# Window attention and a routed expert layer on one core: early gate steps redistributed, the second band's affine sooner, tokens written into the experts' bank by ScalarE

## The reference

```python
x = x + conv_ref(ln_c(x))      # instance norm, qkv, 8x8 windows, 4 heads, softmax, projection
t = to_tokens(x)               # (8, 4096, 32)
t = t + ffn_ref(ln_t(t))       # router softmax over 8 experts, the best 2, weights renormalised
x = from_tokens(t)
```

## Time and profile before

| | |
|---|---|
| time, median of 3 runs | 382.94 us (381.27 to 383.5) |
| time of the profiled execution | 381.23 us |
| its span, first to last instruction | 379.3 us |
| TensorE busy (matmul) | 333.4 us, 88% |
| VectorE busy | 327.5 us, 86% |
| ScalarE busy | 274.8 us, 72% |
| GpSimd busy | 163.6 us, 43% |
| mean granted clock of TensorE | 0.976 |

### The profile page before, as it was taken

The page is one execution under the profiler, slowest core; times in us unless marked ns, Lnnn a source line. Parts: engine busy times, 40 slices in busy tenths (PEclk is TensorE's granted clock), DMA queues, the critical chain, the costliest instruction groups (busy, mean ns, idle before and its releaser), DMA issues.

```text
span 379.3 us, 12902 instructions
## 1 busy us (share of the span) xinstructions
PE 333.4 (88%) x5494; PEld 176.7 (47%) x5494; DVE 327.5 (86%) x422; ACT 274.8 (72%) x477; POOL 163.6 (43%) x191
## 2 busy tenths in 40 slices
PE   7999889999999868989989998989988878858895
PEld 2556556666656534655655654546542212111221
DVE  2599988998998975999998896899898999999884
ACT  3668768779878865787877987876765785566763
POOL 8610000221222120378545212068759448957653
PEclk9999999999999996999999999999999998898999
DMA  7700011011010000101101101075222653773482
GB/s 297 334 3 3 3 31 29 3 31 29 3 32 29 4 14 17 29 2 31 29 3 30 32 2 29 21 174 118 49 65 62 162 129 78 166 182 83 118 210 94
DMA packets 13385, 26.19 MB, mean 69 GB/s; under 512 B 1680, under 2 KB 3856, under 8 KB 12944
## 3 DMA queue, kind: packets, MB, share of 16 engines
q1 hardware_dynamic: 12752, 23.60, 23.7%
q10 hardware_dynamic: 576, 1.77, 1.2%
HBM read 5.96 MB, written 4.19 MB: 27 GB/s over the span
## 4 chain that ended last, share of the span: by engine, by line
PE 50%; DVE 22%; ACT 8%; issue 7%; POOL 6%; DMA 5%; SPq 0%; POOLq 0%; DVEq 0%; ACTq 0%
PE psum L689 13%; PE psum L708 7%; PE psum L674 6%; DVE neg_max L1309 4%; PE psum L716 4%; PE psum L658 3%; PE psum L592 3%; PE psum L869 3%; DVE window_work L1312 3%; PE psum L487 2%; DMA stage<-in_x 2%; PE psum L640 2%; DVE window_work L1466 2%; DVE o_tok L1320 2%; PE psum L859 1%
## 5 line engine op out<-in xcount | busy, mean ns | idle before, releaser
L369 POOL TENSOR_TENSOR o_norm<-o_tok,o_rden 128x128 f32<-128x128 f32 x64 | 25.4, 419 | 169.2 <-DVE o_rden L1322 169.2
L1013 ACT ACTIVATE probs<-psum 128x512 f32<-128x512 f32 x128 | 74.7, 596 | 23.8 <-PE psum L689 23.1
L689 PE MATMUL psum<-weights_sb,window_work 128*128 128x128 f32 x512 | 81.2, 286 | 9.4 <-ACT k_sb L989 5.5
L1309 DVE TENSOR_REDUCE neg_max<-psum 128x16 f32<-128x1024 f32 x64 | 76.8, 1199 | 9.1 <-PE psum L674 9.1
L1312 DVE TENSOR_TENSOR window_work<-psum,neg_max 128x1024 f32<-128x1024 f32 x64 | 78.4, 1225 | 2.2
L689 PEld LDWEIGHTS psum<-weights_sb,window_work 128*128 128x128 f32 x512 | 55.4, 142 | 40.1 <-issue 16.0
L708 PE MATMUL psum<-probs,v_cols 128*32 128x64 f32 x2048 | 52.4, 226 | 0.4 <-DVE o_tok L1320 0.2
L708 PEld LDWEIGHTS psum<-probs,v_cols 128*32 128x32 f32 x2048 | 34.1, 110 | 30.2 <-issue 15.6
L996 ACT ACTIVATE stage<-k_sb,weights_sb 128x512 f32<-128x512 f32 x64 | 44.2, 723 | 0.0
L674 PE MATMUL psum<-stage 32*64 32x256 f32 x1024 | 35.9, 386 | 7.0 <-DVE window_work L1312 4.3
L1320 DVE STREAM_TRANSPOSE o_tok<-psum 128x512 f32<-128x512 f32 x32 | 22.8, 712 | 14.5 <-PE psum L708 14.5
(11 more groups left out here) (143 smaller groups left out, 618.4 us busy)
## 6 DMA issues: line engine op xcount, KB each, us to landing
stage<-act_all SPq DMA_DIRECT2D x36, 256.0 KB, 4.4
out<-v_cols SPq DMA_DIRECT2D x16, 256.0 KB, 2.1
stage<-in_x SPq DMA_DIRECT2D x3, 1024.0 KB, 13.3
x_moved<-x_cur SPq DMA_DIRECT2D x14, 192.0 KB, 2.4
gate_rows<-gate_parts SPq DMA_DIRECT2D x16, 128.0 KB, 2.9
x_moved<-x_cur SPq DMA_DIRECT2D x14, 64.0 KB, 2.2
weights_sb<-weights ACTq DMA_DIRECT2D x1, 811.5 KB, 13.9
stage<-in_x SPq DMA_DIRECT2D x1, 768.0 KB, 6.0
```

Of the source, the lines that this page charges most:

```text
L369: last = pool.tensor_tensor(o_norm[:, hf, :, p * 16:p * 16 + 16].rearrange("p g (b d) -> p g b d", b=2), t[:, p * 8:p * 8 + 8, :].rearrang ...
L689: last = nc.tensor.transpose(bank[TURN_BANKS[v % 2]][:, b * P:b * P + P], heads.rearrange("p h k -> p (h k)"), const["c_ident"][:, :])
L1013: nc.scalar.activation(probs[:, w % 4, :], bank[TURN_BANKS[w % 2]][:, :], ACT.Exp).then_inc(exp_done, 1)
L1309: nc.vector.tensor_reduce(m_t, t, AX.X, ALU.max, negate=True).then_inc(max_done, 1)
```

## The change

Five things are changed.

- Quads 0 and 1 get their own order of gate steps: 17, 18, 19, 20 stand ahead of 16. Steps 2, 19 and 20 go from VectorE to GpSimd. Step 2 is done by GpSimd in chunk 7 (and 13), behind `divide(m - 1, 1)`. VectorE's steps 17 and 18 move from the end of chunk 9 (15) to the place of step 15, between the halves of that chunk; step 24 moves from chunk 10 (and the experts' stage) to the end of chunk 9 (15). GpSimd does 19, 20, 16, 21, 22, 23 in one go in chunk 9 (15), and the copies 25 and 28 and steps 26, 27 and 29 each come half a chunk or a chunk sooner. `gate_exps` stays.
- VectorE's `instance_affine(1)` moves from the end of chunk 6 to behind the first shift of its half 1, and ScalarE's `x_cur` of chunk 8 from the start of chunk 7 to the end of chunk 6.
- TensorE's `queries_keys(m + 1)` moves ahead of one `weigh` (window 5 of chunk m - 1).
- `combine` goes. In all chunks ScalarE writes the tokens into the bank ahead of the experts and copies the result out behind them. `open_bank`, two small matmuls ahead of the last `weigh`, opens bank 6 for that.
- `bias` no longer starts a bank, and waits for the tokens in all chunks.

```diff
GATE_OPS = 30
+        EARLY_ORDER = (*range(16), 17, 18, 19, 20, 16, *range(21, GATE_OPS))
...
-        PRESET_FIRST = 2
...
+        def past(quad, n):
+
+            return (EARLY_ORDER.index(n) if quad < EARLY and n < GATE_OPS else n) + ONE
...
@@ GpSimd @@
             def gates(quad, n):
 
-                pool.wait_ge(gate_step[quad], n + ONE)
+                pool.wait_ge(gate_step[quad], past(quad, n))
                 w = spaces[quad]
-                if n == 5:
+                if n == 2:
+                    pool.wait_ge(raw_done, quad + 1)
+                    follow(pool.tensor_scalar(w.logit, std_two[:, quad % 2, :], const["c_rb"][:, 0:1], None, ALU.mult))
+                    one = pool.tensor_tensor(w.logit, w.logit, raw_logits[:, :], ALU.add)
+                elif n == 5:
...
+                elif n == 19:
+                    one = pool.tensor_tensor(small[:, p_best, :], small[:, near, :], small[:, rden, :], ALU.mult)
+                elif n == 20:
+                    one = pool.tensor_tensor(small[:, p_second, :], small[:, e_gap, :], small[:, p_best, :], ALU.mult)
...
-            EARLY_STEPS = (((5, 6), (8, 9)), ((11, 12, 13, 14), (16,)), ((21, 22, 23), (26, 27)), ((29,), ()))
+            EARLY_STEPS = (((), (2,)), ((5, 6), (8, 9)), ((11, 12, 13, 14), (19, 20, 16, 21, 22, 23)), ((26, 27), (29,)))
...
-                    k = m - (6 * quad + 8)
+                    k = m - (6 * quad + 7)
...
-                    if h == 3:
-                        early(CHUNKS + 1, 0)
...
@@ TensorE, chunk @@
                         turn(m - 1, NW - 1)
+                        queries_keys(m + 1)
                         weigh(*before, NW - 3)
-                        queries_keys(m + 1)
                         weigh(*before, NW - 2)
...
             def bias(c):
 
-                if c < PRESET_FIRST:
-                    wait_past(pe, summed, c - 1)
-                else:
-                    pe.wait_ge(preset, c + 1 - PRESET_FIRST)
-                if c == 1:
-                    pe.wait_ge(x2_done, CHUNKS + X2)
+                pe.wait_ge(preset, c + 1)
...
-                                 start=(c < PRESET_FIRST), stop=False, skip_group_check=True)
+                                 start=False, stop=False, skip_group_check=True)
...
+            def open_bank():
+
+                pe.wait_ge(exp_done, (CHUNKS * NW - 1) + EXP)
+                for half in range(2):
+                    last = nc.tensor.matmul(bank[6][:, half * 2 * P:half * 2 * P + 2 * P], gate_sel[0:32, 0:P],
+                                            gate_sel[0:32, 0:2 * P], start=(half == 0), stop=(half == 1),
+                                            skip_group_check=True)
+                last.then_inc(bank_opened, 1)
+
...
             weigh(CHUNKS - 1, 1, NW - 2)
+            open_bank()
             weigh(CHUNKS - 1, 1, NW - 1)
...
@@ ScalarE @@
                     if (k, hf) == (1, 1):
                         gate_exps(quad)
+                    if (k, hf) == (2, 0):
+                        gate_copies(quad, 25)
                     if (k, hf) == (2, 1):
-                        gate_copies(quad, 25)
-                    if (k, hf) == (3, 0):
                         gate_copies(quad, 28)
...
-                    if hf == 0 and m + 1 == BANDS:
-                        current(m + 1)
...
                         keep_projection(m - 1)
+                    if hf == 1 and m + 2 == BANDS:
+                        current(m + 2)
...
             def preset_bank(c):
 
-                act.wait_ge(summed, c + 1 - PRESET_FIRST)
-                act.wait_ge(x2_done, c + 1 + X2)
+                if c >= 2:
+                    act.wait_ge(summed, c - 1)
+                act.wait_ge(x2_done, (CHUNKS if c == 1 else c + 1) + X2)
...
             exps(CHUNKS - 1, NW - 1)
+            act.wait_ge(bank_opened, 1)
+            preset_bank(0)
             for c in range(CHUNKS):
                 for eh in range(2):
                     copy_gates(c, eh)
+                    if (c, eh) == (0, 0):
+                        early_gates(CHUNKS, 0)
+                    if (c, eh) == (1, 0):
+                        preset_bank(1)
                     if eh == 1 and c >= 1:
-                        if c - 1 >= PRESET_FIRST:
-                            write_out(c - 1)
+                        write_out(c - 1)
...
@@ VectorE @@
-                dve.wait_ge(gate_step[quad], n + ONE)
+                dve.wait_ge(gate_step[quad], past(quad, n))
...
-            EARLY_STEPS = {(6, 8): (0, 1), (7, 8): (2, 3, 4), (8, 1): (7,), (8, 8): (10,), (9, 1): (15,),
-                           (9, 8): (17, 18, 19, 20), (10, 1): (24,)}
+            EARLY_STEPS = {(6, 8): (0, 1), (7, 8): (3, 4), (8, 1): (7,), (8, 8): (10,), (9, 1): (15, 17, 18), (9, 8): (24,)}
...
                     shift(m, hf, 0)
+                    if hf == 1 and m == BANDS - 2:
+                        instance_affine(1)
                     if not first:
                         turn_back(m - 1, hf)
...
-                        elif m == BANDS - 2:
-                            instance_affine(1)
                         early(m, 8)
...
-                    if eh == 0 and 1 <= c <= PRESET_FIRST:
-                        combine(c - 1)
-                    if (c, eh) == (0, 1):
-                        early(CHUNKS, 1)
                     steps(c, eh)
```

More of the change, by code:

```diff
@@ L199, in metaformer_block @@
         preset = sem("preset")
+        bank_opened = sem("bank_opened")
         summed = sem("summed")
@@ L1149, in write_out @@
                 act.wait_ge(y_step, c * 2 + 2)
-                if c == PRESET_FIRST:
-                    act.wait_ge(summed, PRESET_FIRST)
                 wait_past(act, stored[c % OUTS], c // OUTS * 16)
@@ L1181, in _ @@
                         early_gates(CHUNKS, 1)
-                    if (c, eh) == (1, 1):
-                        early_gates(CHUNKS + 1, 0)
                     if eh == 0 and c + REP_FIRST < CHUNKS:
@@ L1438, in _ @@
                 chunk(m)
-            def combine(c):
-                dve.wait_ge(y_step, c * 2 + 2)
-                nc.vector.tensor_tensor(
-                    out_sb[:, c, :].rearrange("p (y win x) -> p win y x", win=NW, y=WS),
-                    bank[6 + c % 2][:, :].rearrange("p (win y x) -> p win y x", win=NW, y=WS),
-                    act_all[:, c * CHUNK:c * CHUNK + CHUNK].rearrange("p (win y x) -> p win y x", win=NW, y=WS),
-                    ALU.add).then_inc(summed, 1)
             divide(CHUNKS - 1, 1)
```

## The result

The changed kernel takes 389.49 us (median of 4 runs, 386.06 to 391.75), the kernel before 382.11 us beside it (4 runs, 381.14 to 383.5): a ratio of 1.0192 with a 95% interval of [1.0144, 1.0241], 7.4 us slower. The forecast was 386.9 us in a range of 381.5 to 391.5. The profiled execution of the changed kernel is the longest of its four, 391.75 us; the profiled one of before took 381.23 us. So the two traces differ by 10.5 us, 3.1 us more than the medians do.

What follows compares the result with a forecast made beforehand. TensorE (88% busy) and VectorE (86%) were taken to bound it by their order of work, VectorE in the experts' stage. Terms -1.0 - 4.3 - 1.3 + 4.0 + 5.1 + 1.3 + 1.8 - 1.65 = +3.95 on 382.94: 386.9 us, range 381.5 to 391.5.

Steps and rivals of the forecast that it cites:

- Part 1: Attention chunks 5, 6, 11 and 12: earlier queries_keys lets a weigh cover the 0.25 us key-copy wait, -1.0 us.
- Part 2: Crossing into the second image group: queries_keys waits 1.9 us in place of 4.0, scores sooner, -4.3 us (-5.0 to -2.1).
- Part 3: Chunks 7 and 13: gate step 2 on idle GpSimd frees 0.65 us of VectorE each time, -1.3 us.
- Parts 4 and 5: Chunks 9 and 15: VectorE's step 17 waits for ScalarE's exp of the gap, holding shift and turn, +4.0 and +5.1 us.
- Part 6: Behind the waits in chunks 9 and 15: TensorE's clock falls to half rate, +1.3 and +1.8 us.
- Part 7: Experts' stage: VectorE loses two combines and step 24, -1.65 us (bounds -2.5 and -0.5).
- (A): Rival: as forecast but the clock falls nowhere, crossing -5.0, sum +0.15, 383.1 us; chance 0.2.
- (B): Rival: experts' stage leaves its low-clock stretches once VectorE is relieved, up to 4.5 us, 378.6 us; chance 0.15.
- (C): Rival: all goes to the worse end, crossing -2.1 and clock behind the waits +5.5, 391.5 us; chance 0.1.

Runs made afterwards that it cites:

- all gate steps as before: Changed kernel with the gate steps back in the places of the kernel before; band, order and bank stay as changed: 374.58 us, 0.9799.
- band and order alone: Kernel before with only the second band sooner and queries_keys one weigh earlier: 376.72 us, 0.9855.
- step 2 alone: Changed kernel with gate steps put back except step 2, which stays on GpSimd; band, order and bank as changed: 373.86 us, 0.9792.
- the kernel with the filler: Changed kernel with four extra fp32 matmuls on TensorE in its waits ahead of turn(9, 4) and turn(15, 4): 384.40 us, 1.0069.
- step 2 alone, again: Second measurement of the changed kernel with gate steps put back except step 2 on GpSimd: 374.15 us, 0.9782.
- step 2, filler, again: Second measurement of the step-2-alone kernel with two extra fp32 matmuls ahead of gate_pair(9, 0, 0): 374.4 us, 0.9785.
- step 2, filler: Step-2-alone kernel with two extra fp32 matmuls ahead of gate_pair(9, 0, 0) in the experts' stage: 372.6 us, 0.9773.
- exp sooner, bank undone: Changed kernel with ScalarE's exp of the gap half a chunk sooner, and bank, bias and combine as before: 376.25 us, 0.9831.
- step 2, bank undone: Step-2-alone kernel with the tokens of chunks 0 and 1 added by VectorE as in the kernel before: 376.15 us, 0.9832.
- gates alone: Kernel before with the redrawn gate steps and nothing else: 393.17 us, 1.0285.
- exp sooner: Changed kernel with ScalarE's exp of the gap half a chunk sooner, in half 0 of chunk 9 (15): 376.82 us, 0.9852.

## Why the prediction came out as it did

The sign and the range were right, and so was the mechanism that it called decisive. The sum came 2.6 us short (386.9 against 389.49). By the differences it is 3.4 us short, +3.95 foreseen and +7.4 measured: the forecast started from 382.94, and the kernel before measured 382.11 with its fourth run. One term is behind it, that of the experts' stage, which had the wrong sign. The others add up to +5.6 as foreseen and to about +5.8 by the traces (-1.0, -5.1, -1.5, +4.4, +5.4 and +3.6), with no error above 0.8 us in one of them.

**Part 1, queries and keys (-1.0).** Right. The waits for k_sb fall from 5.5 us in 13 to 0.9 us in 3, but most of them were no loss. From the first reduce of chunk 0 to that of chunk 6 it is 82.03 us against 82.34, 0.3 us less, and chunks 10 to 14 take 73.31 us with all gate steps as before, against 74.04, 0.7 us less: 1.0 us in all, as foreseen, and far from the 3.5 of the upper bound.

**Part 2, second band (-4.3).** The mechanism is right, with the wait at 2.09 us where 1.9 was worked out and scores at 144.00 where 144.8 was. The size depends on the execution. From chunk 6 to chunk 8 band and order alone gain 5.4 us (32.47 against 37.85), with the clock up, against the -5.0 of one end. In the changed kernel it is 37.85 - 31.99 = 5.9 us, of which about 0.75 us are step 2's. But the clock does not always stay up. The very same kernel, step 2 alone, was profiled twice; the first window is the first profile's, the second that of the other one:

```profile
140.00:143.40 3.40, 3.39 (x80) 1.73 (x64) 3.34 (x5) 2.30 (x4) 0.00 (x0) 1.00 0.00 0
```
```profile
140.40:143.80 3.40, 3.39 (x69) 2.39 (x70) 3.36 (x5) 1.26 (x2) 0.00 (x0) 0.68 0.00 0
```

From chunk 6 to chunk 8 these took 31.71 and 33.41 us, so the half rate costs 1.7 us. It was there in 4 of the 11 profiled executions with the new band, and the length of the wait ahead of queries_keys does not tell them apart (1.79, 1.81, 1.83 and 2.04 us with it, 1.75 to 2.26 us without). The chip may: all three executions on one chip had it, one of the three on a second, none of the four on a third, nor the changed kernel, whose chip is not on record (the two profiles of step 2 alone are from different chips). That was not tested. The value between the two ends is thus no execution in between, but stands for two kinds of them; that it fits the median is luck.

**Part 3, step 2 (-1.3).** By the traces about 0.75 us each time, so 1.5 us where it stands. By the medians 0.7 us, or less in the second measurement (374.58 against 373.86 and 374.15). The cause is right; how much reaches the end, the medians can't tell.

**Parts 4 and 5, the waits (+4.0 and +5.1).** Right, and this is where the forecast was made. Step 17 waits 4.34 us (about 4.0 foreseen) and 4.71 us (4.4), the turns 5.19 (4.9) and 5.80 (5.6). Without the clock, by the kernel with the filler, chunk 9 costs 20.01 - 15.62 = 4.4 us and chunk 15 21.98 - 16.61 = 5.4 us. The turn in chunk 9 was foreseen at 187.9 and came at 181.68 because chunk 9 started 6.5 us sooner; the forecast had kept the times of before and priced the gain apart, which adds up as long as no wait sits against a fixed time. The next reduce started 188.48 - 167.15 = 21.33 us behind the first one. Of the 4.4 us against 4.0, 0.3 us are in the exp of the gap: step 17 was foreseen 11.02 us behind the chunk's first reduce (184.7 - 173.68) and came at 11.35, so the 0.25 us of part 1 did not reach ScalarE here. Step 24 was priced with a wait of 0.5 us for GpSimd. Without the half rate it waits 0.79 us; in the changed kernel, at 187.90, it doesn't wait, only because the half rate had held divide back.

**Part 6, the clock (+1.3 and +1.8).** The half rate came with both waits, and began 1.7 to 1.8 us before their ends. It cost 1.3 us in chunk 9 and 2.3 us in chunk 15, where 1.8 was taken. The range for both together ran from 0 to 5.5, and 3.6 us were measured. The 1.3 was half of a bound and a little more, not a working, and the 1.3 measured are 2.2 us of delay less 0.9 us that came back behind it, most of it at step 24: that they agree is luck. The rule of the Trainium skill (TensorE: Matmul & The Clock Gate, Part 1), that idle time brings the half rate back, held for these two waits, in both kernels that have them without a filler. The price that was put beside it, all matmuls behind the wait at half rate, did not: the clock was back to 0.76 on average in 185.0 to 188.4.

**Part 7, experts' stage (-1.65).** This is the step that failed. In the profiled executions the stage takes 104.7 us against 99.4, +5.3. Since the profiled one is the longest run of its four, the medians give a better estimate, if the time ahead of the gate_pair is the same in all executions: less the 1.8 us outside the span and the time of the gate_pair, 382.11 - 1.8 - 279.95 = 100.4 us before and 389.49 - 1.8 - 285.26 = 102.4 us after, +2.0. Against the forecast that is a miss of 3.65 us. The relief itself is not what failed: the new bank, with the two combines, brings 2.0 and 2.1 us in two comparisons of three. Step 24's share, 0.65 us, was not measured alone. What the sum lacked is that something is lost there at the same time, and it is no part of the new bank: band and order alone, whose experts' stage has the same code as before, lengthens it as well, from 100.4 to 376.72 - 1.8 - 273.15 = 101.8 us by the same estimate.

Two things go with it. One is the clock. The windows from 60 to 70 us behind the first gate_pair, in the kernel before, in band and order alone, and in the changed kernel:

```profile
339.95:349.95 10.00, 8.20 (x46) 1.82 (x46) 9.27 (x14) 6.89 (x12) 8.61 (x7) 0.83 0.40 88
```
```profile
333.15:343.15 10.00, 8.70 (x37) 2.18 (x40) 8.57 (x14) 5.15 (x9) 8.38 (x7) 0.51 0.37 81
```
```profile
345.26:355.26 10.00, 9.20 (x38) 2.04 (x38) 8.57 (x14) 5.84 (x10) 7.88 (x7) 0.50 0.38 85
```

All three lie in the same work, and VectorE, which sets the pace there, does 8.57 us of it in place of 9.27 when the clock is at 0.50. Over the whole stage, us at half rate (within the span) and length of the stage, one profiled execution each:

```
before                      11.4    99.4
step 2 alone                15.1   101.2
step 2 alone, again         17.1   101.8
step 2, filler, again       20.5   101.8
changed, filler in waits    20.5   101.7
band and order              22.0   102.6
step 2, filler              22.2   101.1
exp sooner, bank undone     23.9   104.7
all gate steps as before    23.9   103.1
step 2, bank undone         25.4   104.6
gates alone                 27.3   104.9
exp sooner                  29.2   102.9
changed                     32.7   104.7
```

A microsecond at half rate goes with about 0.25 us more (5.3 us for 21.3), with a scatter of up to 1.7 us either way. The four runs of the changed kernel say the same for one kernel: mean clocks of 0.941, 0.945, 0.956 and 0.964 with 391.75, 390.11, 388.86 and 386.06 us, in order. In the 25 executions of the kernel before that were measured beside the experiments (mean clocks of 0.962 to 0.986, 379.94 to 383.74 us) a straight line through them gives about 0.15 us. But the clock does not account for all of it. At the same mean clock, 0.964, the changed kernel's shortest run takes 386.06 us and the kernel before 381.69 to 382.95. And two runs of band and order alone, at 0.986, have about 10.5 us at half rate in their whole span, while their stage comes to 100.4 and 101.0 us by the estimate above, against 99.4 in the kernel before with 11.4 us. The other thing is one wait, VectorE for the tokens of a late chunk. In the kernel before and in band and order alone:

```profile
DVE window_work L1463 <- DMA stage<-act_all: 1.2, 2, 0.9
```
```profile
DVE window_work L1477 <- DMA stage<-act_all: 2.6, 1, 2.6
```

In the changed kernel it is 0.6 us, so it can't be the cause there. In the other versions it is 1.8 to 3.4 us, and the 3.4 are in the gates alone, whose attention stage is the longest of all, as well as in the changed kernel with the filler: it does not go with the length of the attention stage. Why there is more half rate behind some versions stays open. Two half-rate stretches lie at like places in all thirteen traces, somewhere between 31 and 45 and between 56 and 72 us behind the first gate_pair, a third between 85 and 97 in nine of them, and they vary in length between executions of the same kernel; one attempt to take one away changed the time by nothing that can be seen. What lengthens the stage is thus not found: that the clock is a cause and not only a companion is argued, not shown.

**The rivals.** (A), the clock falls nowhere, is excluded for the two new waits by the windows, and holds for the crossing in 7 of 11 profiles. (B) hung on the experts' stage leaving its low stretches once VectorE is relieved: the opposite came, 32.7 us in place of 11.4. (C) named the worse ends of parts 2 and 6; 2.6 of the 4.6 us that separate it from the forecast came, but by way of part 7, whose upper bound of -0.5 was too low. That the measured time still lies within the range is luck: the room at its upper end was there for parts 2 and 6, and part 7 used it. A bound from the work removed does not bound a stage in which other things can change with it. The bounds were not added up whole either: the low end takes part 1 at -1.0, although its own bound was -3.5, and leaves out the 0.5 us less of part 4.

## What to carry to other kernels

When a step is drawn forward on one engine, look up when each of its inputs is produced on the others, and move the producer too: here the exp of the gap came half a chunk too late, and that one line decides between 389.5 and 376.8 us. Price what is queued behind the waiting step rather than the step, and add a term for the clock where TensorE will wait as long as it did here (5.19 and 5.80 us). And price each part alone: of the four, the redrawn gate steps never paid as a whole, while step 2 alone with the new band, order and bank gives 374 us, 0.978 of the kernel before.

## What the runs showed of the hardware that was not expected

With waits of 1.75 to 2.26 us ahead of queries_keys half rate came in 4 profiled executions of 11, and with those of 5.19 and 5.80 us each time (two kernels, one profile each). Matmuls that compute nothing of use, 3.70 us of them in each wait, held the clock at full rate there and behind, with VectorE's wait as long as before, and the time fell by 5.1 us of 389.5.

A tiny VectorE operation depends on its neighbour. The 128x8 step of instance_affine in the kernel before, and the GpSimd operation that starts with it:

```profile
138.38 1.31 DVE L1224 TENSOR_SCALAR inst_t<-inst,weights_sb 128x8 f32<-128x8 f32 x1
```
```profile
138.40 1.27 POOL L380 TENSOR_TENSOR act_all<-proj_sb,x_win 128x512 f32<-128x512 f32 x1
```

The same step in the changed kernel, where GpSimd has nothing to do (for the first band, at 31.65 us, it takes 0.23 us in the kernel before too, with GpSimd idle):

```profile
130.99 0.23 DVE L1242 TENSOR_SCALAR inst_t<-inst,weights_sb 128x8 f32<-128x8 f32 x1
```

So the affine steps took 0.95 us where the forecast carried over 2.1. The longer time is the length of GpSimd's operation, 1.27 us, and step 20 of the kernel before shows it as well, against the like step ahead of it:

```profile
187.88 0.27 DVE L1386 TENSOR_TENSOR small<-small 128x64 f32<-128x64 f32 x1
188.18 1.20 DVE L1388 TENSOR_TENSOR small<-small 128x64 f32<-128x64 f32 x1
```

GpSimd runs an operation of 1.27 us from 188.02 on. The Trainium skill (SBUF — State Buffer, Who interferes with whom) calls the port pair that VectorE and GpSimd share an exclusive lock held for the whole instruction, by which the loser is blocked outright. The rows agree: both VectorE steps end within 0.1 us of GpSimd's operation (139.69 against 139.67, 189.38 against 189.29), and the trace shows the time as busy, not as a wait. A small step is then worth moving to a place where GpSimd is idle, and its price may not be carried over from where it stood.
